# Third attention: two rows of ones per half written by transfers, smaller clearings placed behind the first quantisation of the phase before

## What is computed

```python
x = x + jnp.tanh(g_ffn[2]) * _L2_ffn_ref(_layernorm(x), L2_ffn_gate_w, L2_ffn_gate_b, ...)
x = x + jnp.tanh(g_xattn[3]) * _L3_xattn_ref(_layernorm(x), ctx_2048, L3_xattn_Wq, ...)

# L2 ffn: "bit linear"
def bit_linear(x, w, b):
    gamma_x = jnp.clip(jnp.max(jnp.abs(x), axis=-1, keepdims=True), 1e-05, None)
    scale_x = 127.0 / gamma_x
    x_dq = jnp.clip(jnp.round(x * scale_x), -128.0, 127.0) / scale_x
    gamma_w = jnp.clip(jnp.mean(jnp.abs(w)), 1e-05, None)
    w_dq = jnp.clip(jnp.round(w / gamma_w), -1.0, 1.0) * gamma_w
    return jnp.einsum('bsd,hd->bsh', x_dq, w_dq) + b
out = bit_linear(silu(bit_linear(x, gate_w, gate_b)) * bit_linear(x, val_w, val_b), out_w, out_b)

# L3 xattn: attention over 256 positions, 8 heads of 8 channels, with rotary embedding
scores = jnp.einsum('bhtc,bhsc->bhts', q, k) / math.sqrt(K_CH)
p_attn = jax.nn.softmax(scores, axis=-1)
out = jnp.einsum('bhts,bhsc->bhtc', p_attn, v)
```

## Time and profile before

| | us |
|---|---|
| median of 3 executions | 1612.32 |
| lowest and highest of them | 1612.14, 1614.03 |
| the profiled execution, its own time | 1609.94 |
| its span in the profile | 1608.1 |

### The profile page before, as it was taken

How to read it: one execution, slowest core, us unless ns; L and a number is a source line. 1 busy time by engine, 2 the same in 40 slices (tenths; PEclk the granted TensorE clock), 3 DMA queues, 4 the chain that set the end, 5 groups by cost and what they waited for, 6 DMA issues and landing times.

```text
span 1608.1 us, 19984 instructions
## 1 busy us (share of the span) xinstructions
PE 1263.4 (79%) x6665; PEld 715.0 (44%) x6670; DVE 1009.5 (63%) x2401; ACT 475.0 (30%) x664; POOL 329.5 (20%) x319
## 2 busy tenths in 40 slices
PE   0127999999979989957777545555898989999997
PEld 0114454545434456635555423222454545456554
DVE  8994353535255256558977789984888888822222
ACT  3462122222103133322222122220454545531110
POOL 2120000000023500023454243334343334000000
PEclk9999999999989999978988656675999999999999
DMA  9100000002000010011101000003232322100001
GB/s 322 30 13 1 0 0 0 0 0 108 1 20 0 14 52 0 1 26 27 26 0 27 3 18 0 0 1 88 88 91 76 90 75 90 41 1 0 0 0 52
DMA packets 67467, 55.68 MB, mean 35 GB/s; under 512 B 23888, under 2 KB 60624, under 8 KB 67152
## 3 DMA queue, kind: packets, MB, share of 16 engines
q1 hardware_dynamic: 66768, 54.67, 11.3%
q10 hardware_dynamic: 640, 0.26, 0.1%
HBM read 39.97 MB, written 14.68 MB: 34 GB/s over the span
## 4 chain that ended last, share of the span: by engine, by line
PE 64%; DVE 19%; issue 11%; ACT 3%; POOL 2%; DMA 1%; DVEq 1%; SPq 0%; POOLq 0%; ACTq 0%
PE banks L1021 7%; PE banks L2030 7%; PE banks L420 6%; PE banks L637 6%; PE banks L416 5%; PE banks L854 3%; PE banks L1028 3%; PE banks L846 3%; PE banks L427 3%; PE banks L431 3%; PE banks L1995 2%; DVE sb_work L1778 2%; DVE sb_work L2268 1%; PE banks L1346 1%; PE banks L1980 1%
## 5 line engine op out<-in xcount | busy, mean ns | idle before, releaser
L2268 DVE TENSOR_REDUCE sb_work<-banks 128x2 f32<-128x512 f32 x256 | 164.7, 685 | 47.0 <-PE banks L1995 44.8
L2139 ACT ACTIVATE sb_work<-banks 128x1024 f32<-128x1024 f32 x128 | 130.9, 1024 | 125.2 <-PE banks L2016 125.1
L537 DVE TENSOR_TENSOR sb_work<-sb_work,banks 128x512 f32<-128x512 f32 x72 | 49.4, 686 | 126.0 <-ACT sb_work L504 126.0
L1459 POOL TENSOR_TENSOR sb_work<-sb_work,sb_consts 128x512 f32<-128x512 f32 x64 | 68.6, 1104 | 247.2 <-ACT sb_work L1403 228.0
L1021 PE MATMUL banks<-sb_work,sb_shelf 128*128 128x512 f32 x256 | 114.4, 592 | 0.0
L420 PE MATMUL banks<-sb_work,sb_shelf 128*128 128x512 f32 (+1 forms) x192 | 92.2, 630 | 8.6 <-DVE sb_work L580 8.6
L997 POOL TENSOR_TENSOR sb_late<-sb_w2n 128x1024 f32<-128x1024 f32 x10 | 22.7, 2267 | 363.1 <-DVE sb_work L691 362.5
L504 ACT ACTIVATE sb_work<-banks 128x512 f32<-128x512 f32 x72 | 42.9, 596 | 181.6 <-PE banks L416 116.2
L637 PE MATMUL banks<-sb_work,sb_ctx_nat 128*64 128x512 f32 (+15 forms) x512 | 89.8, 509 | 7.8 <-DVE sb_work L699 7.8
L1100 DVE TENSOR_TENSOR sb_work<-sb_work,banks 128x512 f32<-128x512 f32 x32 | 22.0, 688 | 112.8 <-ACT sb_work L1086 112.8
L416 PE MATMUL banks<-sb_work,sb_shelf 128*128 128x512 f32 (+1 forms) x192 | 84.9, 593 | 0.0
(11 more groups left out here) (285 smaller groups left out, 2491.6 us busy)
## 6 DMA issues: line engine op xcount, KB each, us to landing
sb_work<-scratch SPq DMA_DIRECT2D x64, 192.0 KB
scratch<-sb_work SPq DMA_DIRECT2D x32, 192.0 KB, 2.1
sb_work<-ctx_t SPq DMA_DIRECT2D x16, 256.0 KB, 4.2
scratch<-sb_work SPq DMA_DIRECT2D x32, 128.0 KB, 2.1
sb_work<-ctx_t SPq DMA_DIRECT2D x4, 512.0 KB, 3.6
sb_ctx_nat<-ctx SPq DMA_DIRECT2D x1, 2048.0 KB, 10.8
sb_raw<-wguT SPq DMA_DIRECT2D x1, 2048.0 KB, 15.2
scratch<-sb_work SPq DMA_DIRECT2D x32, 64.0 KB, 1.8
```

Of the source, the lines that this page charges most:

```text
L1459: ins = nc.gpsimd.tensor_tensor(km_[:, hf, k, :, :], keys.unsqueeze(1).broadcast_to([P, 8, SEQ]), hm2.unsqueeze(2).broadcast_to([P, 8, SEQ ...
L2139: nc.scalar.activation(pt3[:, h % 2, :, :], o, ACT.Exp).then_inc(exp3, 1)
L2268: nc.vector.tensor_reduce(out=mx3[:, tc, k, 2 * hp:2 * hp + 2], in_=bank[u % 2].rearrange("p (h s) -> p h s", h=2), axis=AX, op=ALU.max).t ...
```

## The change

The clearing of all of `kS` goes. In its place two transfers, one for each half, write rows 48 and 49 of the half; their source is a 2 by 64 corner of `groups`, a bfloat16 constant that is one there, read 128 times over. They are started from SyncE behind the `w3T` transfers and counted on `a3_in`, which becomes 19. GpSimd waits for `b_int_ready` 1, the end of the first quantisation of the bit phase, before it sets `bd` to zero and clears `vv0`. SyncE no longer waits for `vv_clear`, and the counts of the two waits for it on VectorE are one lower.

```diff
--- before.py
+++ after.py
@@ -1921,19 +1921,23 @@
                     rows = slice(k * SEQ, (k + 1) * SEQ)
                     sp.dma_start(bd[rows, n, rows], a["w3T"][n, :, :]).then_inc(a3_in, 16)
             for k in range(2):
+                rows = stack_rows(k, MROW + 2)
+                sp.dma_start(kS[rows.stop - 2:rows.stop, :, :, :].rearrange("p i h (n c) -> p (i h n) c", c=SEQ),
+                             groups[0:2, 0:SEQ].unsqueeze(1).broadcast_to([2, BT * H3 * C3 // SEQ, SEQ])).then_inc(a3_in, 16)
+            for k in range(2):
                 sp.dma_start(b3[k * SEQ:(k + 1) * SEQ, :], a["b3"]).then_inc(a3_in, 16)
...
-        A3_DMAS = 17
+        A3_DMAS = 19
 
         def attn3_consts(pool, link, ph):
 
             pool.wait_ge(x_done, updated(max(ph - 1, 0), 0))
+            pool.wait_ge(b_int_ready, 1)
             nc.gpsimd.memset(bd, 0.0).then_inc(bd_zero, 1)
-            nc.gpsimd.memset(kS, 1.0).then_inc(vv_clear, 1)
             clear_values(link, 0).then_inc(vv_clear, 1)
@@ -2178,7 +2182,6 @@
-            sp.wait_ge(vv_clear, 1)
             for m in range(2):
                 for z in range(2):
                     stack(z, m, m)
@@ -2239,7 +2242,7 @@
         def attn3_vector(dve, link, ph):
             dve.wait_ge(a3_in, 16 * A3_DMAS)
-            dve.wait_ge(vv_clear, 2)
+            dve.wait_ge(vv_clear, 1)
@@ -2321,7 +2324,7 @@
                             if isinstance(n, int) and n == 0:
-                                dve.wait_ge(vv_clear, 3)
+                                dve.wait_ge(vv_clear, 2)
                             values(n + 1, (t + 1) % 2)
```

## The result

| | before | changed |
|---|---|---|
| median of 5 executions each, us | 1613.04 | 1606.09 |
| lowest and highest, us | 1612.14, 1614.21 | 1604.77, 1607.81 |
| profiled execution, us (span) | 1609.94 (1608.1) | 1606.97 (1605.2) |
| changed over before | | 0.9957, 95% interval 0.9942 to 0.9971 |

The changed kernel is 6.9 us faster (the interval: 4.7 to 9.4), clear of the 0.2% that can be told from nothing. The forecast was a gain of 7.5 us.

What follows compares the result with a forecast made beforehand. VectorE was taken to bound the bit phase's first quantisation, held by GpSimd clearings. L1122's 5.98 and L1127's 1.50 us, all else zero, gave 7.5 us: 1609.94 to 1602.45 profiled, 1604.8 us on the median's scale, range 1601.1 to 1608.5.

Steps and rivals of the forecast that it cites:

- the likeliest case: Whole program: the forecast of 1604.8 us with its clock range, given a chance of 0.85.
- Part 1: First quantisation of the bit phase: L1122 falls by 5.98 us and the first L1127 by 1.50, together 7.49 us.
- The sum's remark: First quantisation: without the kS clearing but in the old place, the vv0 clearing would still meet it, for up to 2.04 us.
- Part 2: Behind the first quantisation: the moved clearings take 3.10 us and may hold L1814, at no cost to the program.
- the bound of 3.7: Upper bound for L1814's end behind L1129, if the moved clearings hold it: 3.23 + 0.46 us.
- the cover: L1778 starts 4.26 us behind L1129, waiting for TensorE's first product; about 0.6 us left over beside a held L1814.
- Part 3: SyncE's queue: list starts near 923.8 us, two new issues add 1.3 us, transfers take 2 to 10 us, all free.
- Part 5: From L1665 on: same work 7.5 us earlier; granted clock at the third attention's entry taken as zero, ±3.7 us.
- The reading that VectorE ends last in the bit phase: Slices 24 to 27: VectorE is 8 to 9 tenths busy and ends last, so it hands the gain on.
- The moved clearings did not reach the path: Answers the rival that L1814 ends later than TensorE's first product: 3.8 us gained, 1608.5 us, chance 0.07.
- The hold was what made L1122 long: Answers the rival that the first quantisation is slow by itself: 1612.3 us, or 1610.8 with L1127's gain, chance 0.06.
- The third rival: Third attention: TensorE stays at 1.2 GHz longer, rise 21 us later, time 1615.6 us or more, chance 0.02.

Runs made afterwards that it cites:

- e1: Changed kernel without GpSimd's wait for the first quantisation, so bd and vv0 are cleared in the old place; median 1606.36 us, 0.9955 of the kernel before.
- e3: Kernel before, with kS cleared through a float32 view: same bytes, half as many elements; median 1608.05 us, 0.9967 of the kernel before.
- e5: Kernel before, with L1122 written as four scales of one number a partition; median 1609.94 us, 1.0004 of the kernel before.
- e4: Changed kernel, with the clearings waiting for ScalarE's copy of the transposed block, 2.2 us later; median 1604.68 us, 0.9953 of the kernel before.
- e2: Kernel before with only the wait added: all clearings, kS whole, follow the first quantisation; median 1608.45 us, 0.9976 of the kernel before.
- e6: Changed kernel, with GpSimd's output bias addition (L1760) ahead of each block's first product; median 1606.90 us, 0.9970 of the kernel before.
- after_again: The changed kernel run and profiled once more, nothing altered; median 1603.92 us over 12 runs, 0.9955 of the kernel before.
- e7: Changed kernel, with GpSimd waiting between the clearings of bd and vv0; median 1607.15 us, 0.9960 of the kernel before.
- e8: Kernel before with all clearings after the first quantisation, plus GpSimd waits after clearing bd and kS; median 1611.83 us, 0.9992 of the kernel before.

## Why the prediction was right

The median of 1606.09 us lies in the range, 1.3 us above the forecast, and the likeliest case is the one that came. The mechanism was right, as the distance shows. That the median of whole runs came out so near is in part luck: the interval of the gain is 4.7 to 9.4 us, wide against the 0.6 us by which it missed 7.5.

**Part 1, the quantisation.** Right in place and size: 5.98 + 1.50 us forecast, 7.48 and 7.47 us measured in the distance in the two pairs of profiles. e1, e3 and e5 show the cause. The sum's remark that the old place alone would leave up to 2.04 us of hold was an upper bound; e1 measured 1.07, as L1122 came in the middle of that clearing. That share is one of the distance; in the program it can't be seen.

**Part 2, the moved clearings.** L1814 was held, as L1122's row said and L1767's didn't; e5 gives the difference a second time, with 0.34 us for four operations of one number. The page "SBUF — State Buffer" of the Trainium skill, section "Who interferes with whom", was on the side of the hold, and the trace agrees with it: 2817 ns for the first L1814 beside two clearings. On one point the recorded starts don't fit the words of the Trainium skill there, "Whoever issues first": the first L1814 is recorded from 927.51, the clearing of `bd` from 927.60, and the later one went first. A larger lead did win: L1766, a scale of 256 numbers, is recorded in the kernel before from 918.77, 0.14 us ahead of the clearing of `bd`. It took 0.35 us as in the changed kernel, where no clearing runs, and that clearing took 0.88 us in place of 0.74. The pair ended 3.1 us behind L1129, within the bound of 3.7, and the cover had 1.15 us left, not 0.6. e4 shows that the hold was free, e2 what it costs once the clearings outlast the cover.

**Part 3, SyncE.** The start was right: 6.08 us behind L1553, forecast 923.8 − 917.62 = 6.2. The list took 14.4 us, forecast 11.9. The two new issues cost 0.79 us each, and the two of `b3` behind them 3.29 us where before they took 1.23. It was free, as said. The profile doesn't give the landing of the new transfers.

**Part 5, the clock.** This is the term that was mis-sized. I took it as zero with ±3.7 us, placed at the entry of the third attention, and had the bit phase hand the gain on. The two profiles of the changed kernel show more, in every stage: L1553 starts 3.2 us earlier in the second, the stretch from the first L1778 to the third attention takes 150.68 and 153.97 us (150.1 before and forecast), and from VectorE's first scale of the third attention (L2243 before) to its last update of `x` it is 339.1 and 344.4 us. So of the 7.5 us, 6.9 are left at the third attention in the first pair of profiles and 3.65 in the second. The changed kernel's own executions lay between 1598.29 and 1611.56 in the later set of 12. That the median of its first five lay in the range is luck as far as this term goes. A single profiled pair would have shown 2.9 us of the 7.5, and would have been read as half a miss, had the distance not been taken out of it.

**The reading that VectorE ends last in the bit phase** is true for the place of the change, where both other engines stand idle behind it. As a rule for the whole phase e6 doesn't bear it out: 3.85 us of VectorE's time went away there and the stretch did not get shorter.

**The rivals.** The moved clearings did not reach the path (L1778's last wait is for TensorE); e2 is the kernel in which they do. The hold was what made L1122 long. The third rival did not come in the measured profile: the third attention took 339.1 us there and 340.6 and 339.3 in the two profiles of the kernel before. In after_again it took 344.4 us, with a granted clock of 0.86 from 1120 to 1160 us where the first profile had 0.95. So a slower entry does occur, at 5 us and not the 10.7 us that the rival needed, and one profile doesn't show whether the change makes it more frequent.

## What to carry to other kernels

Look in the trace for an instruction whose longest instance is many times its median, and compare its end with the end of what GpSimd does: if the two ends fall together, the cost is the other engine's instruction, and it is worth moving or shrinking even where GpSimd's own time is far off the critical path. Put what is left of it behind a moment after which VectorE has nothing to do until another engine delivers, and add up whether it ends in time. And where the scatter of whole runs is as large as the effect, measure the distance between two instructions around the edit: here it repeated to 0.01 us, while medians moved by 2 and more. Then look at a second pair of instructions a phase further on before calling the difference a gain: here 1.07 us of the distance (e1 against the changed kernel) was gone by there.

## What the runs showed beyond that

- Clearings that follow each other without a wait can keep a VectorE operation out of all of them: L1814 was held 9.68 us through three (e2) and 2.82 us through two, and 0.86 us with a wait between them (e7, e8). In the kernel before and in e3 and e5, the operation that came in the middle of the clearing of `kS` got in at its end, with the next clearing directly behind. What decides between the two, the moment of arrival or another thing, was not tried.
- A clearing costs by its elements, not its bytes: 128 by 8192 bfloat16 took 6.92 us, the same bytes as 128 by 4096 float32 took 3.51 us.
- The stages ahead of the change ended 3.2 us apart in two executions of the very same kernel (922.29 and 919.09), and 9.6 us apart over all kernels, without any difference in the program there.
